# A three-stage decoder layer: weight loads in column blocks, the bias trip and the expert weights on ScalarE's queue

## What is computed

```python
# 1: attention, 32 query heads, 8 key/value heads, head size 64, rotary embedding, causal, sink logits
qkv = layernorm(x) @ qkv_w.T + qkv_b
q, k = rope(q), rope(k)
e = exp(masked(q @ k.T) * scale - m)
w = e / (sum(e) + exp(sink - m))
x = x + (w @ v) @ out_w.T + out_b
# 2: cross attention over features with the context, 8 heads
x = x + softmax(q2.T @ ctx * scale) @ ctx.T          # q2 = layernorm(x), per head
# 3: 8 experts, top 1, and a shared expert
score = sigmoid(top-1 router logit)
routed = down_proj[e] @ (up * silu(gate))            # on layernorm(x) * score
shared = shared_down @ (silu(h @ shared_gate) * (h @ shared_up))
x = x + shared + routed
```

## Time and profile before

| | us |
|---|---|
| median of 3 runs | 1930.46 |
| lowest and highest | 1926.59 and 1932.18 |
| the profiled execution, its own time | 1931.86 |
| its span, first to last instruction | 1930.0 |
| PE busy | 1736.0 (90%) |
| DVE, POOL, ACT busy | 1176.0, 840.1, 820.4 |

### The profile page before, as it was taken

The page is one execution under the profiler, slowest core; times in us unless marked ns, Lnnn a source line. Parts: engine busy times, 40 slices in busy tenths (PEclk is TensorE's granted clock), DMA queues, the critical chain, the costliest instruction groups (busy, mean ns, idle before and its releaser), DMA issues. The chain is left out here.

```text
span 1930.0 us, 45378 instructions
## 1 busy us (share of the span) xinstructions
PE 1736.0 (90%) x15440; PEld 1391.7 (72%) x15441; DVE 1176.0 (61%) x2269; ACT 820.4 (43%) x1575; POOL 840.1 (44%) x1302
## 2 busy tenths in 40 slices
PE   3999999999999999999699899999998588999997
PEld 2787787778778778777577677777775588966664
DVE  5766776676677677667377677777774333422221
ACT  3334443433433434343247666666666233311211
POOL 4544654555465455455234333444434311144443
PEclk9999999999999999999779899999999699999999
DMA  5011111111111111111244344444442265222221
GB/s 178 17 56 45 38 54 54 38 43 54 41 41 54 47 37 52 54 38 40 70 106 107 93 113 109 112 111 114 115 116 71 83 222 175 80 60 69 67 62 40
DMA packets 145343, 148.43 MB, mean 77 GB/s; under 512 B 26194, under 2 KB 139926, under 8 KB 143482
## 3 DMA queue, kind: packets, MB, share of 16 engines
q1 hardware_dynamic: 139514, 133.46, 24.4%
q0 software_dynamic: 5760, 14.06, 2.3%
HBM read 93.46 MB, written 54.11 MB: 76 GB/s over the span
## 5 line engine op out<-in xcount | busy, mean ns | idle before, releaser
L1149 DVE TENSOR_REDUCE xmax<-bankX 128x4 f32<-128x1024 f32 x256 | 310.1, 1217 | 120.1 <-PE bankX L1234 118.6
L1102 ACT ACTIVATE xe<-bankXT 128x512 f32<-128x512 f32 x512 | 292.0, 597 | 107.9 <-PE bankXT L1245 93.1
L1245 PE MATMUL bankXT<-stq,stk 98*128 98x256 f32 x1024 | 229.8, 310 | 19.2 <-DMA stq<-sh 11.5
L369 POOL TENSOR_TENSOR roped<-ropeC,ropeD 128x512 f32<-128x512 f32 x160 | 205.8, 1292 | 57.7 <-DVE ropeD L530 57.6
L557 DVE TENSOR_TENSOR oTl<-bankV,oTh 128x512 fp32r<-128x512 f32 x128 | 88.1, 688 | 199.5 <-ACT oTh L445 199.5
L1245 PEld LDWEIGHTS bankXT<-stq,stk 98*128 98x128 f32 x1024 | 157.1, 192 | 57.9 <-ACT xe L1102 35.0
L662 PE MATMUL bankQ<-wqh,xnTh 128*128 128x512 f32 x384 | 189.7, 494 | 0.0
L1234 PE MATMUL bankX<-stk,stq 96*128 96x256 f32 x1024 | 173.5, 294 | 13.7 <-DMA rw<-in_rw 11.1
L361 POOL TENSOR_TENSOR prob<-prob,rden 128x1024 f32<-128x1024 f32 x64 | 121.9, 1904 | 88.2 <-DVE rden L553 88.2
L1234 PEld LDWEIGHTS bankX<-stk,stq 96*128 96x128 f32 x1024 | 147.4, 199 | 16.6 <-DMA rw<-in_rw 11.3
L662 PE MATMUL bankQ<-wql,xnTh 128*128 128x512 f32 x384 | 152.7, 398 | 0.0
(11 more groups left out here) (196 smaller groups left out, 4045.8 us busy)
## 6 DMA issues: line engine op xcount, KB each, us to landing
stackk_d<-chl SPq DMA_DIRECT2D x96, 128.0 KB, 2.3
stackq_d<-q2hl SPq DMA_DIRECT2D x96, 128.0 KB, 2.3
stk<-stackk_d SPq DMA_DIRECT2D x32, 384.0 KB
stq<-stackq_d SPq DMA_DIRECT2D x128, 96.0 KB
wexp<-in_wexp SPq DMA_DIRECT2D x8, 1536.0 KB
x_d<-x SPq DMA_DIRECT2D x64, 128.0 KB, 1.9
xrden<-inv_d SPq DMA_DIRECT2D x64, 128.0 KB, 2.5
xin<-xg_d SPq DMA_DIRECT2D x40, 128.5 KB
```

Of the source, the lines that this page charges most:

```text
L369: nc.gpsimd.tensor_tensor(roped[c % 3][:], ropeC[c % 2][:], ropeD[c % 2][:], ALU.add).then_inc(s_rsum, 1)
L1102: nc.scalar.activation(xe[q][:].rearrange("p n m -> p (n m)"), bT[:, q % 2, :], ACT.Exp).then_inc(s_xe, 1)
L1149: nc.vector.tensor_reduce(xmax[tile[1] % 2][:, :, a:b + 1:b - a].rearrange("p m h -> p h m"), bS[:, 2 * (pr % 2):2 * (pr % 2) + 2, :].rear ...
L1245: ins = nc.tensor.matmul(bT[:, q % 2, n * D:(n + 1) * D], stk[p][0:98, hd // 4, n * P:(n + 1) * P], stq[p][0:98, hd, :], start=True, stop= ...
```

## The change

Two things are changed.

In attention, `wqkv` is laid out in blocks of 1024 columns, with keys and values in the first (`COL`), so a block serves whole projections. Only the three `wqkv` blocks are loaded at once; the two of `wo` use the buffers of the first two again, and SP waits for their low parts. The bias's loads, writes and read are issued by ACT, at its start. ACT splits blocks 0 to 2 behind `turn_norm` of tile 0, and 3 and 4 (`wo`) at the end of tile 0. DVE makes the low part of block 0 ahead of `turn_rest` of tile 0, of block 1 behind `norm1` of tile 1, of block 2 behind the first rope. POOL makes the low parts of `wo` at the end of its tile 0. PE waits block by block.

In the experts, the eight weights are issued by ACT behind `high_h` of the third unit of groups 0 to 7. The table is worked out in small pieces behind more units, SP takes it on its trip in group 4, and POOL scatters the padding behind the fifth `low_x`.

```diff
-        COL = [NH * HD] + [512 * i for i in range(4)] + [(NH + NKV) * HD]
+        COL = [0] + [1024 + 512 * i for i in range(4)] + [512]
...
             for i in range(NSTAGE):
-                sp.dma_start(stage[:, i, :], wsrc[i]).then_inc(s_stage[i], 16)
+                if i >= 3:
+                    sp.wait_ge(s_lo, i - 2)
+                sp.dma_start(slot[i], wsrc[i]).then_inc(s_stage[i], 16)
...
-            sp.wait_ge(s_brow, 96)
             sp.wait_ge(s_setg, 2)
-            sp.dma_start(bias3[0:3, :], G.bias_d).then_inc(s_brows, 16)
-            sp.wait_ge(s_setg, 1)
...
+                if isinstance(num(tile), int) and num(tile) == 0:
+                    for n in (3, 4):
+                        pool.wait_ge(s_hi, n + 1)
+                        nc.gpsimd.tensor_tensor(wlo[n], raw[n], whi[n].bitcast(F32), ALU.subtract).then_inc(s_loo, 1)
...
         def _(act):
-            for i in range(NSTAGE):
+            nc.scalar.dma_start(bcol[:, 0:24], A["bqkv"].rearrange("(p c) -> p c", c=24)).then_inc(s_bias, 16)
+            nc.scalar.dma_start(bcol[:, 24:26], A["bo"].rearrange("(p c) -> p c", c=2)).then_inc(s_bias, 16)
+            act.wait_ge(s_bterm, 1)
+            for k in range(3):
+                nc.scalar.dma_start(G.bias_d[k, 0:3072].rearrange("(p c) -> p c", c=24), bterm[:, k, 0:24]).then_inc(s_brow, 16)
+                nc.scalar.dma_start(G.bias_d[k, 3072:NBIAS].rearrange("(p c) -> p c", c=2), bterm[:, k, 24:26]).then_inc(s_brow, 16)
+            act.wait_ge(s_brow, 96)
+            act.wait_ge(s_setg, 1)
+            nc.scalar.dma_start(bias3[0:3, :], G.bias_d).then_inc(s_brows, 16)
...
+                if isinstance(num(tile), int) and num(tile) == 0:
+                    high(3)
+                    high(4)
...
                 if front:
                     rope(tile, 0)
+                    if isinstance(t, int) and t == 0:
+                        low(2)
...
             stats1((0, 0))
             norm1((0, 0))
...
+            low(0)
             turn_rest((0, 0))
             stats1((0, 1))
             norm1((0, 1))
+            low(1)
...
+                if isinstance(t, int) and t == 0 and c in (0, 1, 3):
+                    pe.wait_ge(s_lo, (c + 3) // 2)
...
+                if isinstance(t, int) and t == 0 and g == 0:
+                    pe.wait_ge(s_loo, 2)
...
             pe.wait_ge(s_brows, 16)
-            pe.wait_ge(s_lo, NSTAGE)
...
-                if g <= E:
-                    sp.dma_start(wexp[:, (g - 1) * WE:g * WE], A["wexp"][g - 1]).then_inc(s_w, 16)
-                if g == 3:
+                if g == 4:
...
-            for g in range(3):
+            for g in range(5):
                 low_x(g)
             pool.wait_ge(s_pad, 1)
...
+                if n % NF == 2 and n // NF < E:
+                    nc.scalar.dma_start(wexp[:, n // NF * WE:(n // NF + 1) * WE], A["wexp"][n // NF]).then_inc(s_w, 16)
...
-                if n == 0:
+                if n == 1:
                     count_tiles()
+                if n == 2:
+                    sum_tiles()
+                if n == 3:
+                    expert_of()
+                if n == 5:
+                    row_of()
+                if n == 6:
+                    tile_table()
+                if n == 7:
+                    pad_limits()
+                if n in (9, 10):
+                    pad_rows(n - 9)
```

More of the change, by code:

```diff
@@ L185, in attention @@
         kT = sb("kT", [P, NKV // 2, P])
+        with nc.sbuf_tensor("stage2", [P, 2048], F32) as stage2:
+            pass
         prob = sb("prob", [P, 2, 16 * HD + 16])
@@ L423, in evac_v @@
                 act.wait_ge(s_qkv, num(tile) * 6 + 6)
+                if isinstance(num(tile), int) and num(tile) < 2:
+                    act.wait_ge(s_setg, 3)
                 v = bk[1][:, 0, :].rearrange("p (a o d) -> p o a d", o=2, d=HD)
@@ L480, in body @@
                     evac_v(tile)
+                if isinstance(num(tile), int) and num(tile) == 0:
+                    high(3)
+                    high(4)
             turn_norm((0, 0))
+            for i in range(3):
+                high(i)
             tiles(act, body)
@@ L486, in _ @@
         def _(dve):
-            dve.wait_ge(s_const, 16)
-            dve.wait_ge(s_setg, 2)
             def settle(tile):
@@ L536, in shift @@
             def shift(u, r, ch):
+                if isinstance(num(u), int) and num(u) == 0 and r == 0:
+                    dve.wait_ge(s_sinks, 16)
                 dve.wait_ge(s_S, num(u) * 2 + r + 1)
@@ L1472, in _ @@
                     in_=zeros[:], in_offset=None, bounds_check=DUMMY - 1, oob_is_err=False).then_inc(s_padd, 16)
-            for g in range(3, NG):
+            for g in range(5, NG):
                 low_x(g)
```

85 lines of the change are left out of this document (42 added, 43 removed).

## The result

The changed kernel takes **1955.96 us** (median, 1952.32 to 1957.12); the kernel before, run on the same chip, 1930.95. The ratio is 1.012, with a 95% interval of 1.0095 to 1.0146. It is slower by 1.2%, where 1927.7 had been forecast, and it lies far above the 1938 of the range.

A forecast was written before the change was run, and what follows sets the result against it. PE, busy for 90% of the span, was taken as the bound, with only its idle time winnable. Span 1930.0 plus 5.6 (attention) less 8.4 (experts) gave 1927.2, plus 1.86 less 1.40 made 1927.7 us; 8-in-10 range 1917 to 1938.

The forecast's parts named there:

- Only PE's idle time can be won: Whole kernel: PE busy for 90% of the span, the attention loop not edited, so gains only at start and shared-expert groups.
- The start, 6.4 earlier: Kernel start: PE's first projection begins at 21.15 instead of 27.56, because the bias trip starts earlier.
- the bias trip: Kernel start: six small bias writes, first back after 2.15, others 1.2 each, done at 14.4; bounds 9 and 19.
- case D: Kernel start, no gain: writes still wait behind blocks, trip done at 19, PE starts at 25.8; total 1932.3, chance 0.06.
- C: Kernel start, faster rival: writes slow only in the crowd, trip done at 9, PE starts at 15.8; total 1922.3, chance 0.12.
- The 6.75 behind the trip: Kernel start: ACT's and DVE's work for tile 0 between the bias trip's end and PE's start, 6.75 us with hand-overs.
- Tile 0, 4.7: Attention's first tile gives back 4.7 us: 3.0 for project 1, 0.5 before the second rope, 1.2 for `ctx`.
- The term for `ctx`: Tile 0: `ctx` issued 13.4 after PE's start with 2 MB ahead, POOL's split before fourth rope sum; 1.2, bounds 0 to 3.
- Tile 1, 7.3: Attention's second tile gives back 7.3 us: PE stalls 5.7 behind POOL's subtractions, 0.7 more waiting, 0.9 lower clock.
- The experts, 8.4: Shared-expert groups gain 8.4 us: 8.1 from smaller losses around `xs`, scatters and table trip, 0.3 from smaller table pieces.
- Case B: Experts, slower rival: `xs` waits for the block just ahead in all eight groups, 21.6 excess; total 1936.7, chance 0.20.
- shares the time: Experts: `xs` on another queue moves alongside the weight block instead of standing behind it, taking 4.8 us from issue.

The follow-up runs named there:

- e8: Changed kernel with weight blocks 1 and 2 issued only when the six bias writes have landed; 1939.35 us, one run.
- e1: Attention part and weights' layout of the changed kernel, with the experts of the kernel before; 1945.21 us, ratio 1.0087 to the kernel before.
- e3: Changed kernel with 32 unused bytes behind `bterm`, putting attention's buffers on multiples of 64 again; 1942.87 us, ratio 1.007 to the kernel before.
- e5: Changed kernel with tile 0's loads of `ctx`, next `x` and `xres` issued ahead of SP's wait for the first low part; 1942.87 us, ratio 1.0086.
- e7: Changed kernel with ACT's wait for the bias writes and the read put behind the turned rows and high parts of blocks 0 and 1; 1938.1 us.
- e4: Kernel before with 32 unused bytes ahead of `ropeC`, so attention's buffers lie 32 off multiples of 64; 1933.4 us, ratio 1.0035.
- e13: Kernel before with ACT's high part of the next `xs` behind the third unit of a group, not the first; 1919.49 us, ratio 0.9951.
- e6: Changed kernel with the two low parts of `wo` made by DVE at the end of its tile 0, not POOL; 1947.2 us, ratio 1.01.
- e11: Changed kernel with bias read behind high parts of blocks 0 and 1, low parts of `wo` on DVE, and 32 unused bytes; 1935.54 us, ratio 1.0036.
- e12: e11 with `ctx`, next `x` and `xres` of tile 0 issued ahead of the blocks of `wo`; 1937.87 us, ratio 1.0036 to the kernel before.
- e15: e11 with the high parts of `wo` ahead of ACT's first and second evacuation of tile 0; 1930.08 us, ratio 1.0008 to the kernel before.
- e16: Attention of e15 with the experts of e13; 1919.3 us, ratio 0.9964 to the kernel before.

## Why the prediction was wrong, point by point

- **What bounds the kernel**: right for both places. The start and the shared groups were where time could go. "Only PE's idle time can be won" was half of it: of the 20.5 us only 10.3 are idle time, and PE is busy 10.2 longer, by spells at the lower clock and by the loop, which I had set aside as "not edited". Its code is not; its addresses are.
- **The start, 6.4 earlier**: 0.8 in the two traces compared, 0.4 to 2.1 with the others of the same code. The term that failed is the bias trip, done at 19.8 and not at 14.4. I took the rows' 1.2 a write for a write's own time and 2.15 for the first. That reading of the rows was wrong: the first write had landed at 18.30, so the 7.15 us behind 18.26 were five writes at 1.4, and the first had taken 6.95 from its issue. In the changed kernel the first took 6.6 beside three blocks, the others 0.7 to 2.5; beside one block (e8) the trip still took 9.9 against the 9.1 of my sum from the first issue. So of the 5.4 missing, by one trace each, 3.2 are the two more blocks (13.1 less 9.9), 1.4 the later first issue (6.73 against 5.3), and 0.8 slower writes. The upper bound of 19 was nearly it: my case D, in which the writes still wait behind the blocks, had the mechanism, with a chance of 0.06; it is the first write that waits longest. C, a trip done at 9, was not reached even in e8. The 6.75 behind the trip were right (6.9).
- **Tile 0, 4.7**: 9.6. Project 1 came 8.0 after PE's start against 8.2 predicted. The term for `ctx` was mis-sized: 1.2 with bounds of 0 to 3, measured 5.4 of waiting and 2.3 of lower clock behind it. I had the issue time almost right (13.4 after PE's start, measured 14.0) and had named the 2 MB ahead of it, but gave them 1.2 with no row for it. From issue to use it took 8.0 us, behind the second block of `wo` and eight writes of zeros. The wait of 5.41 is the longest among traces of this code: e1 has 3.33 in its place and e3 3.75. The stretch between these two took 0.9 less than before (34.77 to 45.78 against 32.79 to 44.72).
- **Tile 1, 7.3**: 4.6 in the changed kernel, because the wait for `ctx` had already let part of ACT's high parts pass. Where that wait is gone, PE waits 5.25 for POOL's first rope sum (e5, e7), against 5.7 predicted, and the two subtractions take 9.08 against 9.5. The mechanism and its size were right for those kernels; that two waits of the same chain cover each other was missing, and "no other wait covers this" was wrong. In the changed kernel PE doesn't wait for that rope sum at all but 2.39 for DVE, whose step of 16 columns took 3.65 beside POOL's subtractions.
- **Attention in all**: my two tiles give 12.0 of loss behind PE's start, 14.2 were measured. With 0.8 and not 6.4 won at the start and 4.0 lost in the loop, 5.6 becomes 17.4.
- **The loop, nothing**: 3.9, which e4 gets from 32 bytes alone. The step that failed is "not edited". This could have been read ahead of the run from the sizes of the buffers, but no row of before puts a price on it.
- **Cross attention, nothing**: 2.7 in the two traces compared. It holds a spell at the lower clock from 1041 on, with 0.50 granted from 1043 to 1047, 20.3 us for a tile that took 17.3. From the last `mv` of attention to the last `xhl` of cross it takes from 507.3 (e8) to 516.5 us (after) in the nineteen traces, all with the same code there; before has 513.8. I take the 2.7 for this spread, not for the change; what starts the spell wasn't tried.
- **The experts, 8.4**: 0.4. `xs` was used 3.9 to 7.1 us after its issue, where I had 4.8. Case B was right on the mechanism: whatever leaves just ahead is waited for, on either queue, with its 21.6 of excess against 20.5 measured. The rule that I had quoted from the page "DMA: Bandwidth & Descriptors" of the Trainium skill, that another issuing engine saves only the time of the issue, agrees with the trace: 106.9 us against 107.3. I had halved it with "shares the time", with no row for it. `xs` did not share: its packets began when the block's were nearly all started, and it was used 1.5 to 2.0 us behind the start of the last. And I had read the wait for `xs` as a matter of when it lands. It is one of when ACT asks for it, as e13 shows.
- **The chances**: attention's loss and the experts' missing gain each had a case, but I let them stand singly. B and D together, with my own sums for the rest, give 1936.7 + 4.6 = 1941, outside the range; they aren't independent of each other either, since both say that a small transfer waits for the big ones ahead of it.

## What to carry to other kernels

A small transfer waits for the big one issued ahead of it, on whichever queue, so ask first when its reader asks for it: an engine that runs in order should reach for a load at the last point that still serves, and not at the first that it can. Before moving a round trip to the head of an engine's queue, list what stands behind its wait, on that engine and on the queues that wait for it in turn; here the place of that wait was worth 9 to 11 us and the earlier trip itself 1. A buffer of odd size in front of matmul operands can be a change to matmuls that nobody edited.

## What the runs showed of the hardware

- With the weights of its matmuls (`oTh`, `oTl`) moved from a multiple of 64 bytes to 32 bytes off, together with the buffers around them, the group of `project_out` takes 282 ns instead of 279, one start every 120 ns instead of 117, in e4 with nothing else changed. The transposes, whose operands moved as well, stay at 272 ns.
- Six writes, each of 128 pieces of 4 or 48 bytes, took 9.9 us beside one weight block (e8), 12.6 to 13.2 beside three (after, e1, e3, e6) and 14.0 beside five (before); the first alone took 2.7, 6.6 to 6.8 and 6.95. A read of three rows took 2.15 us until PE used it (before), and 4.3 to 5.0 with a block of `wo` beside it (e7, e11, e12, e15, e16).
- A load of 256 KB issued 1.6 to 3.8 us behind a 1.5 MB block on the other queue started its first packet when 6 to 8 of the block's 128 were still to start, in six of eight groups, and was used 1.5 to 2.0 us behind the start of the last, in all eight.
- A DVE step of 0.2 us on 16 columns took 3.65 while POOL subtracted (59.21, above), the same in e1 and e8, and 0.18 in e6, where POOL doesn't subtract.
- The granted clock fell to 1.2 GHz at about 48.2, while PE was idle from 45.78 to 51.19, and rose again at about 58.4.
